# Pre-norm decoder block on one core: context transposes, output weight splits and the prologue's splits of cross attention in another order

## What is computed

```python
q = (text_hidden @ Wq).reshape(B, T_text, 16, 128).transpose(0, 2, 1, 3)
k = (vision_tokens @ Wk).reshape(B, T_vis, 8, 128).transpose(0, 2, 1, 3)
v = (vision_tokens @ Wv).reshape(B, T_vis, 8, 128).transpose(0, 2, 1, 3)
k, v = jnp.repeat(k, 2, axis=1), jnp.repeat(v, 2, axis=1)
scores = jnp.where(mask, jnp.einsum('bhtd,bhsd->bhts', q, k) / scale, -jnp.inf)
out = jnp.einsum('bhts,bhsd->bhtd', softmax(scores), v)
return out.transpose(0, 2, 1, 3).reshape(B, T_text, 2048) @ Wo
```

## Time and profile before

| | us |
|---|---|
| median of 3 runs | 2681.05 |
| lowest and highest | 2679.69, 2681.14 |
| profiled execution, its own time | 2699.72 |
| its span | 2698.0 |
| TensorE (PE) busy | 2495.8, 93% |
| VectorE (DVE), ScalarE (ACT), GpSimd (POOL) busy | 1743.5, 1248.4, 1014.3 |

### The profile page before, as it was taken

The page is one execution under the profiler, slowest core; times in us unless marked ns, Lnnn a source line. Parts: engine busy times, 40 slices in busy tenths (PEclk is TensorE's granted clock), DMA queues, the critical chain, the costliest instruction groups (busy, mean ns, idle before and its releaser), DMA issues. The chain is left out here.

```text
span 2698.0 us, 46191 instructions
## 1 busy us (share of the span) xinstructions
PE 2495.8 (93%) x14850; PEld 2270.3 (84%) x14851; DVE 1743.5 (65%) x4871; ACT 1248.4 (46%) x3155; POOL 1014.3 (38%) x1424
## 2 busy tenths in 40 slices
PE   6999997699999999999999999999999999979388
PEld 5888886589998998999888889989999998969276
DVE  6878886475666657565666657566575656654466
ACT  4545554354544545454554545454454545522211
POOL 3434443043333434343333434344343434431422
PEclk9999999899999999999999999999999999985699
DMA  7322232422121221121132212111121111122654
GB/s 255 95 70 84 93 103 93 142 62 66 56 62 48 87 66 59 55 73 66 49 107 61 82 50 61 50 53 58 41 66 54 41 58 50 44 70 75 217 178 129
DMA packets 110493, 217.89 MB, mean 81 GB/s; under 512 B 20400, under 2 KB 50832, under 8 KB 110016
## 3 DMA queue, kind: packets, MB, share of 16 engines
q1 hardware_dynamic: 105040, 188.42, 22.3%
q0 software_dynamic: 5040, 16.58, 1.6%
q10 hardware_dynamic: 224, 10.49, 1.2%
HBM read 134.57 MB, written 91.36 MB: 84 GB/s over the span
## 5 line engine op out<-in xcount | busy, mean ns | idle before, releaser
L1201 POOL TENSOR_SCALAR x_probs<-x_probs,x_inv 112x376 f32<-112x376 f32 x512 | 634.6, 1249 | 196.0 <-DVE x_inv L1352 196.0
L1245 ACT ACTIVATE x_probs<-x_probs,x_bias 112x376 f32<-112x376 f32 x512 | 307.9, 602 | 426.8 <-POOL x_bias L1195 426.8
L1195 POOL TENSOR_SCALAR x_bias<-x_top 112x1 f32<-112x1 f32 x512 | 118.0, 230 | 973.8 <-DVE x_top L1324 973.8
L1410 PE MATMUL x_ps_f<-x_xT,x_wq 128*128 128x448 f32 x1536 | 342.4, 373 | 7.1 <-DVE x_wq L1292 6.4
L1456 PE MATMUL x_ps_r<-x_wo,x_oT 128*128 128x512 f32 x1344 | 345.6, 393 | 2.3 <-DVE x_wo L1292 1.4
L1410 PE MATMUL x_ps_f<-x_wv,x_ctxT 128*128 128x512 f32 (+1 forms) x1152 | 308.5, 405 | 25.4 <-DVE x_kT L1302 22.8
L1410 PEld LDWEIGHTS x_ps_o<-x_pT,x_v 128*128 128x128 f32 (+1 forms) x2304 | 295.3, 191 | 35.2 <-DVE x_pT L1331 17.4
L1410 PE MATMUL x_ps_s<-x_kT,x_qT 128*112 128x376 f32 x1536 | 313.8, 340 | 3.0 <-DVE x_top L1324 3.0
L1410 PEld LDWEIGHTS x_ps_f<-x_xT,x_wq 128*128 128x128 f32 x1536 | 282.6, 190 | 36.1 <-DVE x_v L1302 6.9
L1410 PE MATMUL x_ps_f<-x_ctxT,x_wk 128*128 128x376 f32 x1536 | 308.7, 337 | 4.2 <-DVE x_kT L1302 3.0
L1410 PE MATMUL x_ps_o<-x_pT,x_v 128*128 128x224 f32 (+1 forms) x2304 | 300.3, 275 | 11.6 <-DVE x_pT L1331 11.6
(11 more groups left out here) (186 smaller groups left out, 3833.6 us busy)
## 6 DMA issues: line engine op xcount, KB each, us to landing
x_ctxs<-x_ctxT SPq DMA_DIRECT2D x32, 752.0 KB, 4.1
x_ctxT<-x_ctxs SPq DMA_DIRECT2D x32, 752.0 KB, 4.7
x_xT<-h2T SPq DMA_DIRECT2D x16, 896.0 KB, 4.9
m_rows<-slots SPq DMA_DIRECT2D x35, 258.0 KB
slots<-w_blank SPq DMA_DIRECT2D x8, 1032.0 KB, 5.2
x_ctxn<-in_ctx_dram SPq DMA_DIRECT2D x32, 256.0 KB
m_hn<-in_L_ffn_W_dram SPq DMA_DIRECT2D x32, 256.0 KB
w_xa<-in_x_dram SPq DMA_DIRECT2D x32, 224.0 KB, 3.5
```

Of the source, the lines that this page charges most:

```text
L1195: pool.tensor_scalar(bias[:, m:m + 1], top[:, m:m + 1], -0.1 * NEG, -SCALE, ALU.max, ALU.mult) \
L1201: pool.tensor_scalar(probs[0:T, m, 0:SE], probs[0:T, m, 0:SE], inv[:, m:m + 1], None, ALU.mult).then_inc(normed, 1)
L1245: act.activation(probs[0:T, m, 0:SE], probs[0:T, m, 0:SE], ACT.Exp, bias=bias[:, m:m + 1], scale=SCALE, accum_out=total[:, m:m + 1]).then_ ...
L1410: last = pe.matmul(out, w, r, start=m == 0, stop=m == len(jobs) - 1)
```

## The change

Four things are moved; the calculation is the same.

1. `late_fills`: both C fills of batch b + 2 are in the third step (g = 2) of batch b. Before, one was in the third and one in the fourth.
2. `splits_at`: the four splits of the output weights of the first half are in batch 1, one per step. Before, they were in batch 0.
3. `HEAD`: the C fills of batch 1 come behind all eight Q fills, just ahead of the first V fill. Before, they stood between the fourth and fifth Q fill.
4. The prologue on ScalarE and VectorE: all four K fills come first, then input chunk c and Q weight piece c in turn, then four Q fills, the V weights, and the rest. The first Q product of a quad on TensorE waits chunk by chunk.

```diff
@@ late_fills
-        if g >= 2 and b + 2 < B:
-            out.append(("C", b + 2, g - 2))
+        if g == 2 and b + 2 < B:
+            out += [("C", b + 2, 0), ("C", b + 2, 1)]
@@ HEAD
-    HEAD = [("C", 0, 0), ("C", 0, 1)] + [("K", 0, g) for g in range(G)] + [("Q", 0, h) for h in range(4)] + \
-           [("C", 1, 0), ("C", 1, 1)] + [("Q", 0, h) for h in range(4, H)] + [("V", 0, 0)]
+    HEAD = [("C", 0, 0), ("C", 0, 1)] + [("K", 0, g) for g in range(G)] + [("Q", 0, h) for h in range(H)] + \
+           [("C", 1, 0), ("C", 1, 1), ("V", 0, 0)]
@@ splits_at
-        if b == 0:
+        if b == 1:
             return [("o", 0, g)]
@@ ScalarE, and the same on VectorE
                 for p in FIRST_SPLITS[0]:
                     split(p)
-                for f in HEAD[0:4]:
+                for f in HEAD[0:6]:
                     fill(f)
                 for c in range(KC):
                     split_x(0, c)
-                for f in HEAD[4:6]:
-                    fill(f)
-                for p in FIRST_SPLITS[1]:
-                    split(p)
-                for f in HEAD[6:-1]:
+                    split(("q", 0, c))
+                for f in HEAD[6:10]:
                     fill(f)
                 for p in FIRST_SPLITS[2]:
                     split(p)
-                fill(HEAD[-1])
+                for f in HEAD[10:]:
+                    fill(f)
@@ TensorE, a Q fill
-                        if n == 0:
-                            weights("q", at * QUAD // B)
-                            pe.wait_ge(x_lo, KC * (at + 1))
-                        last = product(out[:, 0:T4], [(wq[:, a, c, n * D:(n + 1) * D], xT[:, b_, c, :])
-                                                      for c in range(KC) for a, b_ in PASSES])
+                        for c in range(KC):
+                            if n == 0:
+                                weights("q", at * QUAD // B, c)
+                                pe.wait_ge(x_lo, KC * at + c + 1)
+                            for a, b_ in PASSES:
+                                last = pe.matmul(out[:, 0:T4], wq[:, a, c, n * D:(n + 1) * D], xT[:, b_, c, :],
+                                                 start=c == 0 and (a, b_) == PASSES[0],
+                                                 stop=c == KC - 1 and (a, b_) == PASSES[-1])
```

## The result

The changed kernel takes 2670.57 us (median of 8 runs, 2669.47 to 2674.47), the kernel before beside it 2681.1 (8 runs, 2677.56 to 2685.67). The ratio is 0.9961 with a 95% interval of 0.995 to 0.9971: 10.5 us, from 8 to 13. The forecast was 2670.6.

A forecast was written before the change was run, and what follows sets the result against it. TensorE, busy 93% of 2698.0 us, was the bound, leaving its idle time and low-clock matmuls. Gains 3.6 + 3.8 + 3.0 = 10.4 took 2699.72 to 2689.3; less 18.7 for profiling, 2670.6 us, range 2664.5 to 2677.

The forecast's parts named there:

- Part 1: Prologue: weights and input split in turn let the first query product start by quarters; 1.0 us gain, range 0 to 2.5.
- Part 2: Prologue: batch 1's context transposes behind all query products, value weights split earlier; 2.6 us gain, range 2.0 to 3.0.
- Part 3: Batches 0 and 1: output weight splits moved to batch 1 shorten the 5.19 V wait; 3.8 us gain.
- Part 4: Batches 0 to 29: both context transposes in the third step remove V's wait for K; 3.0 us gain, 0 to 5.
- In 3 and 7 the query product behind the pair waits as little for the first transpose's fill: Query batches, third step: the query product's new wait is as small as the 0.15 us put on batch 2's second transpose.
- the exchange of 0.34 for 0.15: Batches 2, 5 and 6: V's 0.34 us fourth-step wait goes, the second transpose waits 0.15 for K instead.
- Batch 29 carries query splits; its waits change place, zero: Batch 29: the transpose pair only moves its waits, so no gain was counted there.
- a whole step more: Context store and load: being issued earlier, they have a whole step more time.
- (a): Rival: clock falls in batches 1, 9, 17 and 25 behind waits of 2.2 us or more, 1.5 each; 2676.6; chance 0.13.
- (b): Rival: weights and input chunks on VectorE make batch 1 so late the output-weight move gains nothing; 2674.4 us; chance 0.12.
- (c): Rival: more gain, as the clock rises with the first query product's quarters and the pair gives 5; 2666 us; chance 0.11.
- (d): Rival: low clock behind third-step second transposes, 2.1 us per fall, eight falls make the kernel slower, 2687.4 us; chance 0.04.

The follow-up runs named there:

- e8: Changed kernel with output weights split behind the third to sixth prologue query fills, value weights two fills earlier, output-weight and third-context loads earlier: 2680.73 us, ratio 0.994.
- e11: Changed kernel with context transposes spread over second and third step, plus the prologue output-weight splits of e8: 2669.37 us.
- e12: e11 with transposes spread only in query batches and batches 1, 9, 17, 25, 29, paired elsewhere: 2668.99 us, ratio 0.9905 to the kernel before.
- e1: Kernel before with only input chunks and query weights split in turn, first query product taken chunk by chunk: 2682.9 us.
- e5: Changed kernel with context transposes single again, in third and fourth step, in query batches and batch 29: 2684.82 us, ratio 0.9953 to the kernel before.
- e6: Changed kernel with the value weights split just ahead of the last fill of HEAD again, behind the last query fill: 2689.62 us.
- e3: Kernel before with only the four output weight splits moved to batch 1: 2675.43 us.
- e2: Kernel before with only batch 1's context transposes behind all query products and value weights split between query fills: 2674.47 us.
- e9: Changed kernel run again without edits, against the kernel before on the same chip: 2683.88 us, ratio 0.996.
- e4: Kernel before with only both context transposes paired in the third step: 2677.19 us.

## Why the prediction was right, and which of its terms were not

The total is right, 2670.57 for 2670.6, and so is most of the mechanism. But the agreement to the last digit is luck: the timed gain is 10.5 with an interval of 8 to 13, two traces of each kernel show 12.4, and terms were off to both sides. The 12.4 are 3.7 in the prologue, 4.4 up to batch 3, 1.6 up to batch 29 and 3.3 up to batch 32, less 0.6 in the second half. The forecast was 3.6, 3.8, 3.0 and nothing for the last two, 10.4.

**Prologue, 3.6 forecast, 3.7 measured.** The split inside it was off. Part 1 (forecast 1.0) is the time from the first context transpose to the fourth query copy: five traces with the old splits take 27.3 to 28.2, on average 27.8, six with the turns 26.6 to 28.3, on average 27.3. That is 0.4, with a scatter of 1.6; e8, e11 and e12, with the value weights two fills earlier, take 26.4 to 27.1. The scatter goes with the clock of the first query matmuls. The changed kernel, on TensorE:

```profile
487.92 0.90 PE L1441 MATMUL x_ps_f<-x_xT,x_wq 128*128 128x448 f32 x3 [3.29 <-DVE x_wq L1290]
489.54 1.49 PE L1441 MATMUL x_ps_f<-x_xT,x_wq 128*128 128x448 f32 x3 [0.72 <-DVE x_wq L1290]
```

The first three matmuls ran at 0.30 us each, in e1 and e5 at 0.49. The quarters start 1.62 to 1.67 apart, close to the 1.72 forecast. The idle times between them are 0.72 and then 0.19 and 0.18 where I had put some 0.6 each, since a quarter at the low clock takes 1.49 to its modelled end and not 1.2. The clock did not rise earlier for the turns: over the 12.3 us from the first query matmul it was 0.72, against 0.78 and 0.81 in two traces of the kernel before, which takes back part of what the earlier start gives. The Trainium skill (TensorE: Matmul & The Clock Gate, "What's actually happening") says that the number of slow matmuls at a start varies between runs of one kernel, and these traces agree: the 0.78 and the 0.81 are of one kernel. Part 2 (forecast 2.6) is 2.8, well inside its range; V starts 1.75 after the last query product where 1.85 was forecast. e6 shows that the transposes' move gains nothing without the earlier value weights.

**Part 3, 3.8 forecast.** The step that was worked out held: the K fill of batch 0's second step ends 9.15 us after the first scores where it ended 12.57 after, 3.4 less for a forecast of 3.5. At batch 3 the move is worth 2.1 alone (1.7 to 2.6) and 3.7 on top of the pair. The argument that the four splits cost batch 1 only what they had cost batch 0 holds with the pair; without it 1 to 2 us come back, with the V wait of 2.70 and the low clock in e3's batch 1. The forecast from the first V product to the K fill in batch 2's third step was 67, measured 66.7 (513.68 to 580.40), in place of 71.1.

**Part 4, 3.0 forecast.** Here two steps failed. "In 3 and 7 the query product behind the pair waits as little for the first transpose's fill": it waits 0.83, seven times, because the pair is over in 0.81 us and by then the first one's fill, a ScalarE copy and a VectorE subtraction, isn't out. Each query batch is 0.58 longer, and e5, with single transposes there, is back at the length of before. And batches 5 and 6 gained 0.42 each, more than the 0.19 of the exchange of 0.34 for 0.15: the second transpose stands right behind the first without a wait, so nothing takes the place of the 0.34. Batches 9, 17 and 25, counted at zero, gain 0.7. In sum the pair gave 1.6 between batches 3 and 29 instead of 3.0. "Batch 29 carries query splits; its waits change place, zero" is the second failure and the larger one: batches 29 to 31 gave 3.3, of which some 1.8 are two falls of the clock that e1, e2 and e3 show can stay away, each in turn, with no edit there. I had not read the row at 1412.94 above; it shows a wait of 2.37 and a V product of 2.82, and the waits that I had listed stop at 1395.

**What was missed.** In batch 0 the pair waits 1.55 for the load of its context. SyncE issues that load at 520.06, behind the loads of the mask and the output weights and a store of the first context, and with part 3 the third step of batch 0 comes 4 us earlier, even with the wait (15.5 us after the first scores for 19.6). The statement that the load of a context has "a whole step more" does not hold there. The wait costs nothing by itself, since in e8 K takes its place. And the clock, which the prediction wanted at 1.00 behind the new waits, did fall behind the 3.16 of batch 1 in one of the two traces.

**The rivals.** (a), a fall of the clock in 1, 9, 17 and 25, did not happen in the changed kernel in 9, 17 and 25 in two traces, but e5, e6 and e8 show that it can, at 1.3 us net each where 1.5 was the price. The argument against it, that VectorE is the chain there and that waits of 1.43 had left the clock alone, is not what kept it away, since e5 has the same chain and the same wait. So the chance of 0.13 was not too high, and that (a) stayed away is luck as far as these runs can tell; with the falls of e5 this kernel would have taken some 5 us more. (b) is refuted by part 3's own runs. (c) and (d) did not come; the 2666 of (c) is also not what its two terms give, 1.5 for the clock and 2.0 for the pair, which is 2667.1.

**The total.** The traces show 12.4 us (two of each kernel), the timed medians 10.5 with an interval of 8 to 13 that holds both. The remaining 2 us between them aren't explained; a single trace moves by that much, and the second comparison, e9, has medians 12.7 apart. The forecast also took 18.7 us off the profiled execution, as a difference that lies elsewhere. The last stage accounts for most of it if it took in the timed runs what it took in the changed kernel's trace (282.9 for 297.3); there is no trace of the kernel before from that chip to show it.

## What to carry to other kernels

With few banks in turn, a product waits for the fill two places before it: put a fill where the one two before is a step old, and write down for each kind of step which it is, since one order is not the best for all (the pair in ordinary batches, spread where other fills or no rows follow). Splits and other side work belong into stretches where the engine that does them idles anyway; the prologue took four output weights at no cost that can be told, and batches 1 and 2 were 4.0 us shorter. Read the waits of every kind of batch down to the last before an edit that touches all of them is summed: 3.3 of the 12.4 us lay behind the one batch whose row was not looked at.

## What was not expected of the hardware

A wait of TensorE of 2.02 us in the same place, with the same instructions around it, was followed by the full clock at 12 of 18 places and by 0.55 to 0.65 of it for the next 3.8 us at the other 6 (batches 9, 17 and 25 in e4, e5, e6, e8 and two traces of the changed kernel), at 1.3 us net a time. Behind a wait of 3.16 one kernel kept the clock in one execution and lost it in another. Behind waits of 2.5 to 2.6 us in the prologue the V product took 1.64 in the two traces of before, e3 and e4, and 2.7 to 2.9 in e1 and e6. The shortest wait behind which it fell in batches 0 to 31 was 1.76 (e3; also 1.77 and 1.78 in e11 and e12), and in five other traces it stayed up behind the same wait; behind single waits of up to 1.66 it never fell there. So in this kernel a wait of 1.8 us or more is a risk that has to be priced, but not one that can be foretold from its length. e12 keeps only two of them, 1.78 in batch 0 and 2.01 in batch 30, and still paid for the first with a fall.
